# A mixture-of-experts layer behind a GNN: two expert blocks from the first five tiles' picks, multiplied during the routing

## The reference

```
xn = layernorm(x)
x  = x + gnn(xn, W, a, src, dst) + mix(xn)       # gnn ends in elu(weighted sum / (row sum + eps))
z  = layernorm(x)
scores = maximum(z @ gate_W + gate_b, 1e-4);  p = softmax(scores)
top 2 experts of each row;  w = maximum(p, 0.1), divided by the sum over the two
out = x + sum over the two picks of w * (z @ expert_W[e] + expert_b[e]) / 2
```

## Time and profile before

| | us |
|---|---|
| three runs | 1190.84, 1191.96, 1192.39 |
| median | 1191.96 |
| the profiled execution | 1190.14 |
| its span, first to last instruction | 1188.3 |
| TensorE matmul busy in the span | 1148.8 |
| VectorE, ScalarE, GpSimd busy | 587.7, 308.7, 462.5 |

### The profile page before, as it was taken

One profiled execution on the slowest core, in us unless ns is written; L12 is line 12 of the kernel. 1 busy time (PEld: TensorE's weight loads), 2 busy tenths in 40 slices (PEclk: granted clock), 3 DMA queues, 4 the chain that ended last, 5 costly groups with the idle time before them and its releaser, 6 DMA issues.

```text
span 1188.3 us, 15152 instructions
## 1 busy us (share of the span) xinstructions
PE 1148.8 (97%) x5588; PEld 984.9 (83%) x5588; DVE 587.7 (49%) x1171; ACT 308.7 (26%) x416; POOL 462.5 (39%) x394
## 2 busy tenths in 40 slices
PE   6999999999999999999999999999959999999996
PEld 5898888888788999999988878888847788788884
DVE  7935666555332122211133447997589622744444
ACT  2421212133111121211022213343353411623232
POOL 0003457457787577511000015233323444443433
PEclk9999999999999999999999999999968999999998
DMA  9382785783634444477457633463288954876653
GB/s 355 114 347 50 204 226 117 232 210 36 137 48 43 93 93 94 97 159 153 92 175 244 204 109 116 166 243 131 94 297 307 336 87 91 257 235 128 190 88 72
DMA packets 115835, 192.15 MB, mean 162 GB/s; under 512 B 33960, under 2 KB 63912, under 8 KB 114624
## 3 DMA queue, kind: packets, MB, share of 16 engines
q1 hardware_dynamic: 81008, 159.53, 39.0%
q0 software_dynamic: 34768, 31.82, 19.8%
HBM read 136.19 MB, written 61.68 MB: 167 GB/s over the span
## 4 chain that ended last, share of the span: by engine, by line
PE 89%; DVE 8%; issue 1%; ACT 1%; DMA 0%; DVEq 0%; POOL 0%; ACTq 0%; POOLq 0%
PE ps L1564 28%; PE ps L1565 28%; PE ps L1566 28%; DVE e_lo L1389 2%; PE ps L1783 2%; PE ps L1712 2%; PE ps L1652 2%; DVE xn_lo L1116 1%; DVE stats L1088 1%; DVE acc L1104 1%; PE ps L1610 1%; DVE y L1534 0%; ACT lt_hi L1012 0%; DMA acc<-in_x 0%; DVE tok_w L1503 0%
## 5 line engine op out<-in xcount | busy, mean ns | idle before, releaser
L734 POOL DMA_INDIRECT cnt_d<-times,addr_i x160 | 263.0, 1644 | 179.1 <-DMA cnt_d<-times,addr_i 96.0
L1564 PE MATMUL ps<-e_hi,lt_hi 128*128 128x512 f32 x368 | 148.0, 402 | 2.8 <-DVE e_lo L1389 2.3
L1566 PE MATMUL ps<-e_hi,lt_lo 128*128 128x512 f32 x368 | 144.1, 392 | 0.0
L1565 PE MATMUL ps<-e_lo,lt_hi 128*128 128x512 f32 x368 | 144.1, 391 | 0.0
L1565 PE MATMUL ps<-xt_lo,q_hi 128*128 128x416 f32 (+1 forms) x384 | 135.0, 352 | 0.0
L1564 PE MATMUL ps<-xt_hi,q_hi 128*128 128x416 f32 (+1 forms) x384 | 135.0, 351 | 0.0
L1566 PE MATMUL ps<-xt_hi,q_lo 128*128 128x416 f32 (+1 forms) x384 | 134.6, 351 | 0.0
L842 POOL DMA_INDIRECT out<-y,row_put x46 | 73.7, 1602 | 87.8 <-ACT y L1046 51.4
L1564 PEld LDWEIGHTS ps<-e_hi,lt_hi 128*128 128x128 f32 x368 | 69.6, 189 | 23.2 <-DVE e_lo L1389 9.0
L1257 DVE TENSOR_TENSOR qs<-ps,qs 128x416 f32<-128x416 f32 (+1 forms) x24 | 14.2, 592 | 136.9 <-PE ps L1566 136.9
L1566 PEld LDWEIGHTS ps<-e_hi,lt_lo 128*128 128x128 f32 x368 | 69.5, 189 | 14.9
(11 more groups left out here) (257 smaller groups left out, 2382.0 us busy)
## 6 DMA issues: line engine op xcount, KB each, us to landing
e_raw<-in_L_ffn_expert_W SPq DMA_DIRECT2D x64, 512.0 KB, 9.8
cnt_d<-zeros SPq DMA_DIRECT2D x20, 640.0 KB, 12.2
rows<-key_d SPq DMA_DIRECT2D x8, 1250.0 KB, 7.5
acc<-in_x SPq DMA_DIRECT2D x18, 512.0 KB, 7.5
w_raw<-in_L_mix_w_key SPq DMA_DIRECT2D x16, 512.0 KB, 4.4
cnt_d<-cnt_d POOLq DMA_DIRECT2D x10, 640.0 KB, 7.6
cnt<-cnt_d SPq DMA_DIRECT2D x10, 640.0 KB, 5.9
h_d<-hs SPq DMA_DIRECT2D x18, 256.0 KB, 2.3
```

Of the source, the lines that this page charges most:

```text
L734: nc.gpsimd.indirect_dma_start(out=cnt_d[i], out_offset=bass.IndirectOffsetOnAxis(ap=addr_i[:, j:j + 1], axis=0), in_=times[:, j:j + 1], i ...
L1564: nc.tensor.matmul(o, lh, rh, start=(k == 0), stop=False)
L1565: nc.tensor.matmul(o, lh, rl, start=False, stop=False)
L1566: return nc.tensor.matmul(o, ll, rh, start=False, stop=(k == last_k))
```

## The change

The loop over experts gets a ninth turn in front, the expert that most picks of the first five tiles go to.

- **VectorE** makes the first five tiles' choice (`early_choice`) ahead of tile 7's rows, behind a wait for `tri2`. After tile 7 come `early_places` (the commonest expert as an index, `early_e`, and the places of its first 256 picks), after tile 8's row sum `early_tokens`, after tile 8's rows `early_taken`, which takes these picks out of the later count. The late choice covers tiles 5 to 9.
- **TensorE** gets two more jobs in the rotation of banks: `early_totals` between the halves of tile 8, `early_rows` ahead of tile 7's transposes. Ahead of the last gate it transposes the first early block; `early_part` multiplies both blocks in pieces of 4 or 2 rows of weights (12 or 6 matmuls) between the waits of the routing, into banks 0, 1 and 3, 2.
- **SP** waits for the index in the GNN's last tile, loads it and the chosen expert's rows by it. Nine experts are loaded, the chosen one twice.
- **GpSimd** makes counters and triangle earlier, issues two gathers for the early blocks, and takes over eight of the weights' subtractions (`chosen_lo`): rows 4 to 7 of the chosen expert and rows 0 to 3 of expert 0. The second set stands ahead of the gather of the second regular block and of `out_seen`. Both early blocks are scattered ahead of its loop.
- `s_mm`, `s_ye`, `s_tr` and the slots count on: the early blocks are 0 and 1, expert 0's block is 2.

```diff
-    NBLK = (TOPK * N + NE * P) // P
+    TE, EARLY = 5, 2
+    FULL = TE * P * TOPK // NE
+    NBLK = EARLY + (TOPK * N - FULL + NE * P) // P
+    NV = NE + 1
...
             if t == NT - 1:
+                early_rows_job = len(owner)
+                owner.append("dve")
                 tr_jobs(NT - 3)
...
+            if t == NT - 2:
+                early_tot_job = len(owner) + 1
+                owner.extend(["act", "dve", "act", "dve"])
...
# SP
-                if t == 4:
-                    sp.wait_ge(s_full, first["GNN"])
-                    load_expert(0, range(MB))
+                if t == NT - 1:
+                    sp.wait_ge(s_early, CHOSEN)
+                    chosen = sp.value_load(early_e[0:1, 0:1], min_val=0, max_val=NE - 1)
+                    load_chosen(chosen, range(MB))
...
# GpSimd
+                if t == NT:
+                    for i in range(2):
+                        pool.wait_ge(s_xn2d[i], 16 * len(range(i, TE, 2)))
+                    pool.wait_ge(*released(early_rows_job))
+                    gather_early(0)
...
+            pool.wait_ge(s_tr, 2)
+            gather_early(1)
+            def chosen_lo(v, rows):
+                for k in rows:
+                    pool.wait_ge(s_ehi, KB * v + k + 1)
+                    nc.gpsimd.tensor_tensor(e_lo[v % NLO][k][:, :], e_raw[v % NLO][k][:, :], e_hi[v % 2][:, k, :].bitcast(f32),
+                                            ALU.subtract).then_inc(s_elop, 1)
+            chosen_lo(0, range(FIRST_LO, KB))
...
-            gather_rows(tok_of[:, 0:1])
+            pool.wait_ge(s_tr, 2 * EARLY)
+            gather_rows(tok_of[:, EARLY:EARLY + 1])
             pool.wait_ge(s_non, 1)
             pool.wait_ge(s_pre, 1)
...
+            chosen_lo(1, range(FIRST_LO))
+            pool.wait_ge(s_tr, 2 * EARLY + 2)
+            gather_rows(tok_of[:, EARLY + 1:EARLY + 2])
             pool.wait_ge(s_rows, NH)
             for h in range(NH):
 ...
+            for i in range(EARLY):
+                for h in range(NH):
+                    c = slice(h * HALF, (h + 1) * HALF)
+                    pool.wait_ge(s_sc[h], i * 16 + 16)
+                    nc.gpsimd.tensor_copy(row_put[:, h:h + 1], row_of[:, h, i:i + 1]).then_inc(s_put, 1)
...
+                    nc.gpsimd.indirect_dma_start(out=out.rearrange("n (h c) -> (n h) c", h=NH),
...
-            with pool.Fori(0, blocks) as i:
+            with pool.Fori(EARLY, blocks) as i:
...
# VectorE, behind the routing
+            dve.wait_ge(s_bias[0], 16)
+            for i in range(EARLY):
+                for h in range(NH):
+                    dve.wait_ge(s_y[h], i + 1)
+                    dve.wait_ge(s_mm, i * 3 + (1 + 2 * h))
+                    V.tensor_tensor(yb[:, c], ps[:, EARLY_BANKS[i][h], :], bias[0][:, c], ALU.add).then_inc(s_ye, 1)
+                if i == 0:
+                    dve.wait_ge(s_wslot, 1)
+                right_weighed(i)
+                if i == 0:
+                    expert_lo(1, range(FIRST_LO, KB))
...
# TensorE
+            pe.wait_ge(s_gx, 16)
+            for g in range(2):
+                block_transposes(g, bank=EARLY_TR)
             gate(NT - 1)
+            early_part(0, 0, range(MB))
+            early_part(0, 1, range(MB // 2))
             pe.wait_ge(s_gtot, 1)
             nc.tensor.matmul(ps[:, 7, 0:NE], tri2[:, :], g_tot[:, :], start=True, stop=True)
...
+            pe.wait_ge(s_gx, 32)
+            pe.wait_ge(s_llo, 2)
+            for g in range(2):
+                block_transposes(g)
+            early_part(0, 1, range(MB // 2, MB))
+            for h in range(NH):
+                early_part(1, h, range(MB))
...
             last.then_inc(s_tokp, 1)
+            early_part(0, 0, range(MB, KB))
+            pe.wait_ge(s_route, 1)
             pe.wait_ge(s_non, 1)
             nc.tensor.matmul(ps[:, 6, 0:NE], tri2[:, :], pad_n[:, :], start=True, stop=True).then_inc(s_nonp, 1)
+            early_part(0, 1, range(MB, KB))
+            pe.wait_ge(s_gx, 48)
+            pe.wait_ge(s_llo, 4)
             for g in range(2):
                 block_transposes(g)
+            early_part(1, 0, range(MB, KB))
...
             last.then_inc(s_padp, 1)
+            early_part(1, 1, range(MB, KB))
-            for e in range(NE):
-                with pe.Fori(first_block[e], first_block[e + 1]) as i:
+            for v in range(1, NV):
+                with pe.Fori(first_block[v], first_block[v + 1]) as i:
```

More of the change, by code:

```diff
@@ L1021, in _ @@
             gate_in(NT - 1)
+            for g in range(2):
+                block_hi(0, g, bank=EARLY_TR)
             expert_hi(0, range(FIRST_LO, KB))
@@ L1449, in _ @@
             V.tensor_tensor(g_pos[:, :, :], g_run[:, :, :].rearrange("p e t -> p t e"), over_tiles(g_place[:, :]), ALU.add).then_inc(s_gpos, 1)
+            for g in range(2):
+                block_lo(1, g, lt2_hi, lt2_lo)
             dve.wait_ge(s_gpos, 1)
@@ L1512, in _ @@
             for g in range(2):
-                block_lo(0, g)
-            expert_lo(0, range(FIRST_LO, KB))
+                block_lo(EARLY, g)
             dve.wait_ge(s_padp, 1)
@@ L1540, in _ @@
                         dve.wait_ge(s_mm, i * 3 + (1 + 2 * h))
-                        V.tensor_tensor(yb[:, c], ps[:, h, :], bias[e % NBIAS][:, c], ALU.add).then_inc(s_ye, 1)
-                        if h == 1 and e == NE - 1:
+                        V.tensor_tensor(yb[:, c], ps[:, h, :], bias[v % NBIAS][:, c], ALU.add).then_inc(s_ye, 1)
+                        if h == 1 and v == NV - 1:
                             right_weighed(i)
                         block_lo(i + 1, h)
-                        if h == 1 and e < NE - 1:
+                        if h == 1 and v < NV - 1:
                             right_weighed(i)
-                if e + 1 < NE:
-                    expert_lo(e + 1, range(AHEAD[e], KB))
+                if v + 1 < NV:
+                    expert_lo(v + 1, range(AHEAD[v], KB))
         @block.tensor
@@ L1751, in _, with block_transposes, early_part @@
                         rows_transposed(t - 2)
+            def block_transposes(g, bank=4):
+                for b in range(MB):
+                    k = MB * g + b
+                    last = nc.tensor.transpose(ps[:, bank + g, b * P:(b + 1) * P], gx[:, k * P:(k + 1) * P], ident[:, :])
+                last.then_inc(s_tr, 1)
+            def early_part(i, h, rows):
+                hi, lo = (lt_hi, lt_lo) if i == 0 else (lt2_hi, lt2_lo)
+                c = slice(h * HALF, (h + 1) * HALF)
+                for k in rows:
+                    if k % MB == 0:
+                        pe.wait_ge(s_llo, i * 2 + (k // MB + 1))
+                    pe.wait_ge(s_ehi, k + 1)
+                    pe.wait_ge(*lows_done(0, k))
+                    last = three(ps[:, EARLY_BANKS[i][h], :], hi[:, k, :], lo[:, k, :], e_hi[0][:, k, c], e_lo[0][k][:, c], k, KB - 1)
+                    if k == KB - 1 or (h == 1 and k == KB - 2):
+                        last.then_inc(s_mm, 1)
             nodes_half(NT - 1, 0)
```

372 lines of the change are left out of this document (249 added, 123 removed).

## The result

The changed kernel takes 1211.94 us (median of 4 runs, 1210.95 to 1213.29), the kernel before beside it 1191.4 us: ratio 1.0174, interval 1.0157 to 1.0192. It is 20.5 us slower, where the prediction had 14 us slower.

What follows compares the result with a forecast made beforehand. TensorE's work and its idle time in the routing were taken as the bound. A loop start 38.3 us later, minus 23.6 for two saved blocks and 1.0 for pacing, gave +13.7 on 1191.96: 1206 us, range 1193 to 1214.

Steps and rivals of the forecast that it cites:

- the third rival: Transfers at the early blocks also late, scatters landing slowly amid weight loads: 4 to 6 us more, 1211 us; chance 0.15.
- three signs of being wrong: Bias adds before 920, GpSimd's subtractions taking 1.2 us, or out_seen issued before 912 would show the forecast wrong.
- Taken away: Expert loop: two blocks fewer, by the count of picks, at 11.8 us each: 23.6 us off.
- Term 1: Last GNN tiles: early choice and two inserted bank jobs delay tile 9's first half: +3.7 us.
- Term 2: Last gate: eight transposes of gathered rows stand ahead of it, 1.9 us with 0.6 hidden; +5.0 together with the GNN delay.
- Term 3: Late choice: GpSimd's subtractions take turns with VectorE's short steps, so g_tot comes later: +6.8 us.
- Term 4: From g_tot to the tokens: inserted transposes, splits and 30 partly hidden early matmuls: +3.6 us.
- Term 5: Behind the tokens: pad steps, register load, four GpSimd subtractions and out_seen's landing put the loop's start at 934.8.
- The moved counters: Token tables' counters moved to GpSimd in tile 1: costed at nothing, since the delayed rows are wanted much later.
- Pacing: First two loop blocks: the second runs somewhat shorter, about 13.0 us: -1.0 us.
- the first (port no hindrance): Late choice and behind: GpSimd doesn't hinder VectorE, loop starts at 924, +3 us, 1195 us; chance 0.14.
- The second: Loop start: TensorE's own work decides, start at 908 to 910, 10 us faster, 1181 us; chance 0.09.

Runs made afterwards that it cites:

- e6: Kernel before, with only the four subtractions of expert 0's rows 4 to 7 moved from VectorE to GpSimd: 1198.10 us, ratio 1.0053.
- e4: Changed kernel, with the chosen expert's four subtractions (rows 4 to 7) on VectorE instead of GpSimd: 1208.19 us, ratio 1.0126.
- e5: Changed kernel, with the next expert's four subtractions (rows 0 to 3) on VectorE instead of GpSimd: 1202.46 us, ratio 1.0090.
- e3: Changed kernel, with the out_seen transfers issued before the token table's steps on GpSimd: 1206.37 us, ratio 1.0119.
- e11: e10, with all early bias adds and the first weighing ahead of the next expert's subtractions on VectorE: 1198.97 us, ratio 1.0065.
- e12: e11, with tile 8's two short sum steps taken inside the early table on VectorE: 1196.12 us, ratio 1.0036.
- e1: Kernel before, with only the token tables' counters made in tile 1 on GpSimd, in the changed kernel's memory: 1197.66 us, ratio 1.0038.
- e10: e8, with the loop's second expert's first five roundings and subtractions ahead of the second early block's weighing: 1199.17 us, ratio 1.0060.
- e8: Changed kernel, counters in tiles 4 to 6, out_seen first, both subtraction sets on VectorE, second early block's bias adds ahead of rows 4 to 7: 1197.07 us.

## Why the prediction was right, and where it was off

The sign, the range and the mechanism held: a queue on GpSimd and VectorE, with out_seen and four subtractions in it, sets the loop's start, later than the two saved blocks are worth. The range held with 2 us to spare. The measured 1211.9 lies above the forecast's own band of 1199 to 1209 and next to the third rival's 1211, which is luck: that rival's 4 to 6 us of late transfers are 2.3 us here, and most of the difference is a term that stood at nothing. The size was 6.5 us short on the medians (20.5 against 14) and 9.5 us short in the pair of profiles (23.2 against 13.7). None of the three signs of being wrong appeared: the first early bias adds are at 928.99, GpSimd's subtractions took 2.3 us and more, and out_seen was issued at 929.97. Point by point, from the pair of profiles:

- **Taken away, 23.6:** 23.3 measured, with 21 blocks (336 matmuls of each kind in the loop and 32 before it, 368 in all).
- **Term 1, +3.7:** 3.8 measured from tile 8's transposes to the start of tile 9 (859.26 - 837.28 against 849.69 - 831.50). Not foreseen was that TensorE would begin tile 9 at the low clock: 1.6 us more up to the end of the GNN (875.00 - 859.26 against 863.78 - 849.69).
- **Term 2, +1.3:** 1.4 measured, from there to the last gate's sums (12.97 against 11.53 us).
- **Term 3, the port, +6.8:** 6.3 measured in the changed kernel, 5.9 in e6 alone. It was worked out from one overlap of 1.52 us and one of 1.59, and e4 and e6 show it from both sides. The price isn't fixed: from the last gate's sums to g_tot the choice takes 3.6 us in e4, where GpSimd doesn't subtract, 10.5 in the changed kernel and 12.1 in e5.
- **Term 4, +3.6:** 5.0 measured. The 30 early matmuls ahead of the token sums were taken as partly hidden. They aren't: TensorE starts them after the transposes, at 901.59 on the chain, needs 8.0 us, the first six at the low clock, and the sums start only at 909.59.
- **Term 5, +22.9 from the tokens to the first block:** 22.6 measured. The pad steps took 6.8 (7), the register load that no row had priced 0.3 on the chain (0.8), the four subtractions ended at 928.78, 10.7 us behind their start (10.8 with the turns), the landing took 6.7 on the chain (4.4), and the start of the first block came 31.6 us after tok_of. e3 and e5 show both halves: the place of out_seen, and the four subtractions. TensorE was idle for 11.15 us ahead of the loop, less than the 12 to 18 foretold: it did the last 12 early matmuls only when pad_c was there, from 926.84 to 931.9, and not by 918.
- **The moved counters, at nothing:** 5.8 us. This is the step of the prediction that failed. The prediction said that in tile 1 TensorE is never idle and that the rows "are wanted much later"; both are so at tile 1. But VectorE's and ScalarE's pipeline starts a tile every 14.5 us and doesn't make up 3 us, and at tile 3, where TensorE first needs gate rows of ScalarE, only 0.67 us of slack are left. The text even named the loss of that cover (up to 3.5 us) and didn't follow it; the rest is the clock.
- **Pacing, -1.0:** not seen; with the 23.3 instead of 23.6 this makes 1.3 us.

So 9.5 = 5.8 (counters) + 1.6 (clock in tile 9) + 1.4 (term 4) + 1.3 (loop) - 0.6 (terms 1 to 3 and 5 together).

Of the rivals, the first (port no hindrance) is refuted by e6. The third (transfers late too) was right in that the landing took 2.3 us longer than taken, and wrong in that this was one of small terms. The second named the condition (a start below 920.1) and no kernel here met it and kept its loop: e11 and e12 start at 919.7 and 919.0, and give 8.5 to 9.0 us back in the loop.

What stays open: why the low clock after TensorE's wait at tile 3 lasts for ten matmuls in one execution and fewer in another (the gate group at 784.27 in e3 and 784.44 in e5, 785.74 to 785.99 in the changed kernel, e1 and e4, which are alike up to there), and why it comes at all behind the wait of 1.23 us at tile 9 in some executions and not in others (transposes of 1.94 us in the changed kernel, 1.06 in e5 and e10); whether the counters in one piece would cost nothing one tile later; and whether a loop whose scatters don't wait for one another would let the early start through. The last two weren't tried.

## What to carry to other kernels

Work moved to an idle engine has three prices that its own duration doesn't show: what is queued behind it there (a transfer's issue of 1 us waited 10.7 us behind four subtractions), whose short steps it locks out while it runs (0.2 us steps became 2.0 to 2.3, and one 8.7), and, in a paced pipeline, a delay that is handed on from tile to tile until some engine runs out of slack. Before a piece goes "where nobody waits", follow the engine's next item to its consumer, two or three tiles on, and put the piece where the engine is idle for longer than it takes (5.45 us in tile 1 were too few for 8.5). And before you win an earlier start, ask what paces the steps behind it: four microseconds of start were worth nothing here, because the next weights' subtractions stood behind weighings that wait for landings.

## What the runs showed of the hardware

- **GpSimd and VectorE lock each other out for whole instructions.** GpSimd's four subtractions of 128x1024 take 9.35 us, 2.34 each, in e5, where no step of VectorE that waits comes between, and the same in the changed kernel, where four do; beside VectorE's 16-bit products they take 10.68, 2.67 each. VectorE's two-input steps of 0.2 us last to the end of the one under way (2.0 to 2.3 us); its reductions pass. A one-input TENSOR_SCALAR of 128x40, 0.18 us in e4, waits too: 1.22 us in the changed kernel, to the end of one subtraction, and 8.68 us in e5, to the end of all four.
- **A short wait costs TensorE more than itself.** Behind 2.3 us of waiting at tile 3 part of the gate, the transposes and some nine matmuls ran at 1.2 GHz: 5.6 to 5.8 us in all in the changed kernel and in e1, 4.1 in e3's execution, where gate and transposes kept the full clock.
- **Landings.** out_seen landed 5.4 to 6.7 us behind its issue amid the weight loads (before, changed kernel), and a scatter on the changed kernel's chain 9.1 us behind its own (941.56). Weighings that each wait for the block before to land stood 10.8 to 11.0 us apart (e8, e10, e11).
